# Reordering SyncE's transfers and the tap order of row-tiled matmuls in a deformable convolution kernel

## The chip, the cores and the metric
The kernel runs on one core of one Trainium2 chip. The time is that of one execution on the device, in microseconds, as a median over runs.

## What is computed
The input x has 8 images of 32 channels and 128x128 pixels, float32. Two blocks are applied one after the other, each to the group-normalised x (32 groups of one channel, so mean and variance of each channel of each image), and each adds its result to x.

```python
x  = x  + L0(_gn(x))    # depthwise 3x3, then three channel mixes (two of them softmax matrices)
x1 = x
x  = x1 + L1(_gn(x1))
# L1: off = conv3x3(v, w_off)               64 channels: a row and a column offset per pixel and channel
#     mapped = bilinear sample of v at grid + off, clipped to the image
#     conv3x3(mapped, w_conv) + b_conv
```

## The kernel before
**Stages.** L0 is folded into one 3x3 convolution, conv1, whose result x1 stands in `x1a` (three buffers, one per image in turn). Then come the offsets (`offsets`), the sampling in 8 chunks of an image (`deform` on VectorE, `offset_parts` on ScalarE, the chunk loop on GpSimd), and conv2 on the sampled image, which VectorE adds to `x1a`; from there it is stored. The image index is i, a step s takes two of the 8 chunks, so an image has four steps.

**TensorE.** In each step it first runs `offsets(i, s)` and then the jobs of `jobs_behind`: conv1 of image i+1 in steps 0 and 1 (four groups each, `x1`), conv2 of image i-1 in steps 2 and 3 (`c2`). A job waits in `wait_freed` until the PSUM bank that it takes has been read. The fourth conv1 group takes the bank of the first. In images 0, 1 and 7 the jobs are spread in another way.

**Offsets (L801 to L823).** A matmul takes one row group r (32 partitions of x1a, one image row in four) and one half t of the output's partitions, so there are eight tiles (r, t). For each of three ky, nine taps in all, kx is the outer loop and the rotated row groups are the inner one. At ky > 0 the row group r adds to what r - 1 wrote, so L813 waits for that row group's last matmul of the ky before, on one of four semaphores.

**SyncE's queue, in program order (L554 to L617).** For image i: copy mapa's first half to mapb (`copy_mapb(0)`, 2 DMAs); store half 1 of image i-2 (4 DMAs, L461 and L464); move the sampled rows of half 1 into mapa (`move_mapa(1)`, 16 DMAs) and copy them to mapb; load xb of image i+2 (8 DMAs); wait for x1's pads and move both halves of image i+1's strips (`move_strips`, 16 DMAs a half); `move_mapa(0)`, as soon as conv2 of image i-1 has done four groups; store half 0 of image i-1 (5 DMAs) after six groups were added. An image's first conv2 group waits for both halves of mapa and mapb (L765 to L769).

**What hangs on it.** `x1_group` (L957) must not overwrite `x1a` before the image that it held is stored: group 0 of image i+1 waits for half 0 of image i-2. `clamp(i, 1)` fills the borders of the strips' half 1 and `row_steps(i, 2)` and `(i, 3)` on GpSimd subtract its rows; chunks 4 to 7 read them. `STORE_AFTER` is the count of added groups at which a half may be stored, `CONV2_GROUPS` the order of conv2's groups; group g writes blocks 4g to 4g+3 of 32, and half 0 of mapa is what the even groups read.

Of the kernel before, what the change touches and what calls it, by code (L numbers as in the profile page):

```python
# [13 lines left out]
def deformable_preact_kernel(nc, x, dw_w, pw_w, att_w, glob_w, off_w, conv_w, conv_b, out):  # L14
# [15 lines left out]
    NK = HQ // KR  # L30
# [17 lines left out]
    NS = NK // 2  # L48
# [9 lines left out]

    BANKS = ["", "c", "xc", "xyc", "cxyc", "ycxyc"]

    CONV2_GROUPS = [0, 2, 4, 6, 1, 3, 5, 7]
    STORE_AFTER = [6, 8]
    BEFORE_END_GROUPS = [1, 2, 3, 0, 4, 5, 6, 7]


# [5 lines left out]
    def spread(i):  # L71
        return isinstance(i, int) and NB - 2 <= i < NB
# [77 lines left out]
    with ctx:  # L150
# [6 lines left out]
        def sem(name):  # L157
            return ctx.enter_context(nc.semaphore(name))
# [134 lines left out]
        mapped_pads = sem("mapped_pads")  # L293
# [13 lines left out]
        first2_done = sem("first_group_of_conv2_done")  # L307
        x1_ready = sem("x1_ready")
        off_done = [sem(f"off_done_side{n}") for n in range(2)]
        row_step = [sem(f"row_step_of_rows{n}") for n in range(4)]  # L310
        off_used = sem("off_used")
        parts_ready = sem("parts_ready")
        cols_ready = sem("cols_ready")
# [5 lines left out]
        mapped_ready = sem("mapped_ready")  # L319
        conv2_done = sem("conv2_done")  # L320
# [118 lines left out]
        def move_strips(queue, i, half):  # L439
            for strip in range(4):  # L440
                move_strip(queue, i, half, strip)
# [33 lines left out]
        def _(sp):  # L475
# [27 lines left out]
            def move_mapa(half):  # L503
                move_rows(mapa, 4 * half, 4, mapa_moved[half])
# [49 lines left out]
            for i in range(NB):  # L554
                prev, nxt, after = i >= 1, i + 1 < NB, i + 2 < NB
                if prev:

                    if i == 1:
                        move_strips(sp, i, 1)
                    sp.wait_ge(map_pads, i)  # L560
                    sp.wait_ge(mapa_moved[0], A_MOVES * DMA * i)
                    copy_mapb(0)
                if nxt and i >= 2:
                    sp.wait_ge(out_ready, 8 * (i - 1))
                    store(sp, i - 2, (i - 2) % 3, 1)
                if prev:
                    sp.wait_ge(mapped_ready, NK * i)
                    if i >= 2:
                        sp.wait_ge(conv2_done, 8 * (i - 1))
                    sp.wait_ge(mapped_pads, 2 * i)  # L570
                    move_mapa(1)
                    sp.wait_ge(mapa_moved[1], A_MOVES * DMA * i)
                    copy_mapb(1)
                if after and prev:
                    for half in range(2):

                        sp.wait_ge(conv1_done, 8 * (i + 1) + (5 if half == 0 else 8))
                        load_xb(i + 2, half, xb_loaded)
                if not prev:
                    sp.wait_ge(mapped_ready, 4)  # L580
                    sp.wait_ge(s_setup["dve"], 6)
                    sp.wait_ge(mapped_pads, 1)
                    move_mapa(0)
                if nxt:

                    sp.wait_ge(x1_pads, i + 2)
                    sp.wait_ge(mapped_ready, NK * i + 4)
                    for half in range(2 if prev else 1):
                        move_strips(sp, i + 1, half)
                if not nxt:  # L590
                    if i >= 2:
                        sp.wait_ge(out_ready, 8 * (i - 1))
                        for part in range(2):
                            store(sp, i - 2, (i - 2) % 3, part)
                    sp.wait_ge(end_pads, 1)
                    sp.wait_ge(mapped_pads, 2 * i + 1)
                    sp.wait_ge(mapped_ready, NK * i + 4)
                    move_rows(xa, 0, 4, end_moved[0])
                    sp.wait_ge(end_moved[0], A_MOVES * DMA)
                    copy_rows(xb, xa, 0, 4, end_copied)  # L600
                    sp.wait_ge(mapped_pads, 2 * i + 2)
                    sp.wait_ge(mapped_ready, NK * i + 6)
                    move_end_rows((0, 1), FULL, end_moved[1])
                    sp.wait_ge(mapped_ready, NK * i + 7)
                    move_end_rows((2, 3), LEFT, end_moved[1])
                    sp.wait_ge(out_ready, 8 * i)
                    for part in range(2):
                        store(sp, i - 1, (i - 1) % 3, part)
                    break
                if prev:  # L610
                    sp.wait_ge(mapped_ready, NK * i + 4)
                    sp.wait_ge(conv2_done, 8 * (i - 1) + 4)
                    sp.wait_ge(mapped_pads, 2 * i + 1)
                    move_mapa(0)
                if prev and after:
                    sp.wait_ge(out_ready, 8 * (i - 1) + STORE_AFTER[0])
                    store(sp, i - 1, (i - 1) % 3, 0)  # L617


            for m in (1, 3, 5):  # L620
# [48 lines left out]
        def _(pe):  # L669
# [131 lines left out]
            def offsets(i, wpar, par, s, tiles):  # L801


                half, parity = s // 2, s % 2
                for ky in range(3):
                    order = [(3 + ky + n) % 4 for n in range(4)]
                    for kx in range(3):
                        for r in order:
                            c = (r - ky) % 4
                            side, n, shift = c % 2, c // 2, (c + ky) // 4  # L810
                            if ky > 0 and kx == 0:

                                pe.wait_ge(row_step[(r - 1) % 4], 4 * (NS * i + s) + 2 * ky)  # L813
                            for t in range(2):
                                b = 2 * NJ * t + NJ * half + parity + shift
                                last = nc.tensor.matmul(tiles[side][64 * t:64 * t + 64, CH * n:CH * n + CH],  # L816
                                                        wo[wpar][Q * r:Q * r + Q, 3 * ky + kx, :],
                                                        x1a[par][Q * r:Q * r + Q, b:b + 7:2, kx:kx + W],
                                                        start=(ky == 0 and kx == 0), stop=(ky == 2 and kx == 2))
                                if kx == 2 and ky < 2:  # L820
                                    last.then_inc(row_step[r], 1)
                                elif kx == 2:
                                    last.then_inc(off_done[side], 1)  # L823

# [44 lines left out]
        def _(act):  # L869
# [193 lines left out]
            for i in range(NB):  # L1063
                prev, nxt = i >= 1, i + 1 < NB
                for s in range(NS):
# [25 lines left out]
                    sum_far(i, b)  # L1091
                    if s == 0:
                        pad_mapped(i, i % 3, 0)
                        clamp(i, 1)
                    if s == 1 and not nxt:
                        pad_end(i % 3)
# [53 lines left out]
        def _(pool):  # L1150
# [62 lines left out]
            for i in range(NB):  # L1213
                for k in range(NK):
# [20 lines left out]
                    if i >= 1 and k % 4 == 0:  # L1235
                        pool.wait_ge(mapa_moved[k // 4], A_MOVES * DMA * i)
                    pool.tensor_tensor(mapped_of_chunk(k), split(side), split(column),  # L1237
                                       ALU.add).then_inc(mapped_ready, 1)
                    if k in (1, 3):
                        row_steps(i, 2 + k // 2)  # L1240
                    elif k >= NK - 2 and i + 1 < NB:
                        row_steps(i + 1, k % 2)

# [379 lines left out]
```

## Time and profile before
| what | value |
|---|---|
| median of 3 runs | 734.21 us (733.68 to 735.55) |
| profiled execution | 738.19 us, span on the core 736.3 us |
| granted TensorE clock, mean | 0.959 of full |
| TensorE, VectorE, GpSimd, ScalarE busy | 89%, 72%, 65%, 61% of the span |
| chain that ended last | TensorE 39%, SyncE's queue 21%, ScalarE 7%, VectorE 6% |
| offsets (L816) | 4608 matmul records, 289.2 us busy |

L12 is line 12 of the kernel. PEld is TensorE's loading of weights. SPq is SyncE issuing DMAs: the engine is held while it issues one. Every matmul of float32 shows as two records, each with its own weight load, so the 72 matmuls of a block of offsets are 144 records. PEclk is the granted share of TensorE's full clock of 2.4 GHz. The ends of matmuls are modelled, so their starts are what to read.

### The profile page before, as it was taken

The page shows a single profiled execution, that of the slowest core. Times are in us where ns is not written, and L with a number is a line of the kernel's source. Part 1 is how long each engine was busy: PE and PEld are TensorE (multiplying, and loading weights), DVE is VectorE, ACT ScalarE, POOL GpSimd, SP SyncE. Part 2 cuts the span into 40 slices and gives each one's busy share as a digit, 9 for nine tenths or more (in the row PEclk, how much of TensorE's full clock was granted, in tenths as well). Part 3 has the DMA queues.
Part 4 walks back from the last instruction along what each step waited for, and adds up shares of the span by engine and source line. Part 5 has one row for each costly group of instructions (what it writes and reads, how often), then busy time and mean ns, then how long its engine had stood idle before and what let it go on. Part 6 is the DMA issues. An engine that isn't in the chain of part 4 may idle for free.

```text
span 736.3 us, 16859 instructions
## 1 busy us (share of the span) xinstructions
PE 655.6 (89%) x6572; PEld 297.2 (40%) x6572; DVE 528.4 (72%) x1027; ACT 451.1 (61%) x778; POOL 478.8 (65%) x412
## 2 busy tenths in 40 slices
PE   4799877888996999889997999989997999789965
PEld 4334433344442444434442444433443444344422
DVE  3686987558894688828886488848987386567872
ACT  7236757676754766556665766548656666576740
POOL 4013746969687476857768376876768476977650
PEclk9999999989998999989998999999999999989989
DMA  8958723589348894498747894498945623457555
GB/s 143 186 112 152 117 59 75 137 165 160 75 105 192 176 171 115 120 210 164 141 107 168 179 201 103 106 208 174 154 114 140 145 60 77 106 126 184 128 125 130
DMA packets 135413, 101.40 MB, mean 138 GB/s; under 512 B 13696, under 2 KB 112544, under 8 KB 135328
## 3 DMA queue, kind: packets, MB, share of 16 engines
q1 hardware_dynamic: 111296, 88.47, 57.6%
q10 hardware_dynamic: 24032, 11.78, 9.6%
q8 instruction: 54, 0.88, 0.6%
q14 instruction: 31, 0.25, 0.1%
HBM read 31.59 MB, written 16.78 MB: 66 GB/s over the span
## 4 chain that ended last, share of the span: by engine, by line
PE 39%; SPq 21%; ACT 7%; DVE 6%; issue 5%; POOL 5%; DMA 2%; ACTq 1%; DVEq 0%; POOLq 0%
PE off_ps L816 21%; SPq L429 11%; PE c_ps L698 9%; PE off_ps L698 7%; SPq L500 7%; DMA out_dram<-x1a 2%; DVE other_row L1426 2%; ACT off_abs L1010 2%; SPq L461 1%; ACT down_ps L1008 1%; ACT beyond L1020 1%; ACT other_row L997 1%; SPq L464 1%; DVE xb L1504 1%; POOL other_col L1231 1%
## 5 line engine op out<-in xcount | busy, mean ns | idle before, releaser
L816 PE MATMUL off_ps<-x1a,wo 32*64 32x512 f32 x4608 | 289.2, 611 | 22.6 <-ACT x1a L965 12.4
L816 PEld LDWEIGHTS off_ps<-x1a,wo 32*64 32x64 f32 x4608 | 162.1, 133 | 149.8 <-issue 65.7
L1426 DVE COPY_PREDICATED other_row<-down_ps,row_diff 128x768 f32<-128x768 int32 x128 | 124.6, 1027 | 117.5 <-ACT down_ps L1008 117.5
L997 ACT ACTIVATE other_row<-row_diff 128x768 f32<-128x768 f32 x128 | 101.1, 839 | 57.9 <-POOL row_diff L1207 26.3
L1223 POOL TENSOR_TENSOR other_row<-other_row,x_strips 128x512 f32<-128x512 f32 x48 | 57.2, 1192 | 118.2 <-DVE other_row L1440 118.2
L1224 POOL TENSOR_TENSOR other_col<-other_col,other_row 128x512 f32<-128x512 f32 x64 | 87.8, 1372 | 43.6 <-DVE other_row L1440 43.6
L1008 ACT ACTIVATE down_ps<-off_ps,bias_o 128x512 f32<-128x512 f32 x64 | 42.0, 655 | 100.3 <-PE off_ps L816 85.9
L698 PE MATMUL off_ps<-xb,w 128*64 128x512 f32 x198 | 90.3, 605 | 8.2 <-DVE xb L1504 7.0
L698 PE MATMUL c_ps<-xb,w 128*64 128x512 f32 x138 | 74.5, 682 | 22.0 <-ACT x1a L965 22.0
L700 PE MATMUL off_ps<-xa,w 128*64 128x512 f32 x198 | 90.3, 605 | 0.0
L1231 POOL TENSOR_TENSOR other_col<-other_col,off_abs 128x512 f32<-128x512 f32 x64 | 82.8, 1294 | 5.0
L698 PE MATMUL off_ps<-mapb,w 128*64 128x512 f32 x192 | 85.9, 595 | 0.0
L1228 POOL TENSOR_TENSOR other_col<-other_col,other_row 128x512 f32<-128x512 f32 x64 | 81.9, 1279 | 5.0
L1237 POOL TENSOR_TENSOR mapped<-other_col,other_row 128x512 f32<-128x512 f32 x64 | 81.7, 1277 | 5.0
L1205 POOL TENSOR_TENSOR row_diff<-x_strips 128x792 f32<-128x792 f32 x32 | 52.9, 1653 | 45.9 <-ACT x_strips L1039 45.9
L700 PE MATMUL off_ps<-mapa,w 128*64 128x512 f32 x168 | 75.0, 595 | 0.0
L1020 ACT ACTIVATE beyond<-off_abs,minus_one 128x1024 bf16<-128x1024 f32 x64 | 73.3, 1145 | 2.0
L700 PE MATMUL c_ps<-xa,w 128*64 128x512 f32 x138 | 74.5, 682 | 0.0
L1010 ACT ACTIVATE off_abs<-off_ps,bias_o 128x1024 f32<-128x1024 f32 x64 | 71.0, 1110 | 0.0
L698 PE MATMUL c_ps<-mapb,w 128*64 128x512 f32 x144 | 65.9, 593 | 0.0
L1382 DVE BATCH_NORM_STATS2 stats<-x1a 128x6 f32<-128x512 f32 x64 | 40.7, 681 | 34.7 <-ACT x1a L965 34.7
L700 PE MATMUL c_ps<-mapa,w 128*64 128x512 f32 x126 | 57.7, 593 | 0.0
(160 smaller groups left out, 1059.9 us busy)
## 6 DMA issues: line engine op xcount, KB each, us to landing
mapa<-mapped SPq DMA_DIRECT2D x224, 65.0 KB, 2.1
mapb<-mapa SPq DMA_DIRECT2D x28, 520.0 KB, 6.4
out_dram<-x1a SPq DMA_DIRECT2D x49, 256.0 KB, 4.7
xb<-in_x_dram SPq DMA_DIRECT2D x48, 256.0 KB, 10.6
xa<-in_x_dram ACTq DMA_DIRECT2D x40, 256.0 KB, 7.4
x_strips<-x1a SPq DMA_DIRECT2D x112, 81.2 KB, 2.1
x_strips<-x1a SPq DMA_DIRECT2D x112, 65.0 KB, 2.0
xa<-in_x_dram SPq DMA_DIRECT2D x16, 256.0 KB, 6.5
```

The costliest lines, as they stand in the source:

```text
L429: queue.dma_start(to[p_to:p_to + Q, at:at + n * WP], x1a[par][p:p + Q, b:b + n, :].rearrange("p b w -> p (b w)")) .then_inc(strips_loaded[ ...
L698: nc.tensor.matmul(bank[0:64, :], weights[:, kx, :], rows_b[:, of, kx:kx + W], start=(kx == 0), stop=(kx == 2))
L700: last = nc.tensor.matmul(bank[64:128, :], weights[:, kx, :], rows_a[:, of, kx:kx + W], start=(kx == 0), stop=(kx == 2))
L816: last = nc.tensor.matmul(tiles[side][64 * t:64 * t + 64, CH * n:CH * n + CH], wo[wpar][Q * r:Q * r + Q, 3 * ky + kx, :], x1a[par][Q * r:Q ...
L997: act.activation(other_row[n][:, :, KR // 2 * odd:KR // 2 * odd + KR // 2, :], diff_of_chunk(k, odd), ACT.Copy)
L1010: act.activation(off_abs[n][:, :], off[:, :], ACT.Abs, bias=bias_o[i % 2][:, 0:1]).then_inc(abs_ready, 1)
L1020: act.activation(beyond[:, :], off_abs[k % 2][:, :], ACT.Relu, bias=minus_one[:, :], accum_out=far[i % 2][:, k:k + 1]).then_inc(beyond_rea ...
L1224: step(pool.tensor_tensor(side, side, other_row[n][:, 0, :, :], ALU.add))
L1228: step(pool.tensor_tensor(side, side, column, ALU.subtract))
L1231: step(pool.tensor_tensor(side, side, off_abs[n][:, 1:2 * CH:2].rearrange("p (h w) -> p h w", h=KR), ALU.mult))
L1237: pool.tensor_tensor(mapped_of_chunk(k), split(side), split(column), ALU.add).then_inc(mapped_ready, 1)
L1426: last = dve.copy_predicated(other_row[n][:, :, KR // 2 * odd:KR // 2 * odd + KR // 2, :], bass.AP(tensor=rows.tensor, offset=rows.offset ...
```

## The change
SyncE: half 1 of the strips is no longer moved along with half 0 at the end of the image before, but in the image itself, after the store of image i-2. At the end of the iteration the store of half 0 now comes ahead of `move_mapa(0)`; the store waits for four added groups and not six, `move_mapa(0)` for six groups of conv2 and not four. conv2's groups come in an order that finishes half 0 of the image first. ScalarE does `clamp(i, 1)` at the end of step 1 and not of step 0, and GpSimd `row_steps(i, 2)` after chunk 2 and not chunk 1. TensorE: for each ky one wait for all eight tiles, on one semaphore, and then for each row group all three kx for both t.

```diff
--- before.py
+++ after.py
@@ -58,8 +58,9 @@
 
     BANKS = ["", "c", "xc", "xyc", "cxyc", "ycxyc"]
 
-    CONV2_GROUPS = [0, 2, 4, 6, 1, 3, 5, 7]
-    STORE_AFTER = [6, 8]
+    CONV2_GROUPS = [0, 2, 1, 3, 4, 6, 5, 7]
+    STORE_AFTER = [4, 8]
+    HALF_READ = 6
     BEFORE_END_GROUPS = [1, 2, 3, 0, 4, 5, 6, 7]
 
 
@@ -307,7 +308,7 @@
         first2_done = sem("first_group_of_conv2_done")
         x1_ready = sem("x1_ready")
         off_done = [sem(f"off_done_side{n}") for n in range(2)]
-        row_step = [sem(f"row_step_of_rows{n}") for n in range(4)]
+        row_step = sem("row_step")
         off_used = sem("off_used")
         parts_ready = sem("parts_ready")
         cols_ready = sem("cols_ready")
@@ -554,9 +555,6 @@
             for i in range(NB):
                 prev, nxt, after = i >= 1, i + 1 < NB, i + 2 < NB
                 if prev:
-
-                    if i == 1:
-                        move_strips(sp, i, 1)
                     sp.wait_ge(map_pads, i)
                     sp.wait_ge(mapa_moved[0], A_MOVES * DMA * i)
                     copy_mapb(0)
@@ -564,6 +562,7 @@
                     sp.wait_ge(out_ready, 8 * (i - 1))
                     store(sp, i - 2, (i - 2) % 3, 1)
                 if prev:
+                    move_strips(sp, i, 1)
                     sp.wait_ge(mapped_ready, NK * i)
                     if i >= 2:
                         sp.wait_ge(conv2_done, 8 * (i - 1))
@@ -585,8 +584,7 @@
 
                     sp.wait_ge(x1_pads, i + 2)
                     sp.wait_ge(mapped_ready, NK * i + 4)
-                    for half in range(2 if prev else 1):
-                        move_strips(sp, i + 1, half)
+                    move_strips(sp, i + 1, 0)
                 if not nxt:
                     if i >= 2:
                         sp.wait_ge(out_ready, 8 * (i - 1))
@@ -607,14 +605,13 @@
                     for part in range(2):
                         store(sp, i - 1, (i - 1) % 3, part)
                     break
-                if prev:
-                    sp.wait_ge(mapped_ready, NK * i + 4)
-                    sp.wait_ge(conv2_done, 8 * (i - 1) + 4)
-                    sp.wait_ge(mapped_pads, 2 * i + 1)
-                    move_mapa(0)
                 if prev and after:
                     sp.wait_ge(out_ready, 8 * (i - 1) + STORE_AFTER[0])
                     store(sp, i - 1, (i - 1) % 3, 0)
+                if prev:
+                    sp.wait_ge(conv2_done, 8 * (i - 1) + (4 if spread(i - 1) else HALF_READ))
+                    sp.wait_ge(mapped_pads, 2 * i + 1)
+                    move_mapa(0)
 
 
             for m in (1, 3, 5):
@@ -803,14 +800,13 @@
 
                 half, parity = s // 2, s % 2
                 for ky in range(3):
-                    order = [(3 + ky + n) % 4 for n in range(4)]
-                    for kx in range(3):
-                        for r in order:
+                    if ky > 0:
+
+                        pe.wait_ge(row_step, 16 * (NS * i + s) + 8 * ky)
+                    for r in range(4):
+                        for kx in range(3):
                             c = (r - ky) % 4
                             side, n, shift = c % 2, c // 2, (c + ky) // 4
-                            if ky > 0 and kx == 0:
-
-                                pe.wait_ge(row_step[(r - 1) % 4], 4 * (NS * i + s) + 2 * ky)
                             for t in range(2):
                                 b = 2 * NJ * t + NJ * half + parity + shift
                                 last = nc.tensor.matmul(tiles[side][64 * t:64 * t + 64, CH * n:CH * n + CH],
@@ -818,7 +814,7 @@
                                                         x1a[par][Q * r:Q * r + Q, b:b + 7:2, kx:kx + W],
                                                         start=(ky == 0 and kx == 0), stop=(ky == 2 and kx == 2))
                                 if kx == 2 and ky < 2:
-                                    last.then_inc(row_step[r], 1)
+                                    last.then_inc(row_step, 1)
                                 elif kx == 2:
                                     last.then_inc(off_done[side], 1)
 
@@ -1091,6 +1087,7 @@
                     sum_far(i, b)
                     if s == 0:
                         pad_mapped(i, i % 3, 0)
+                    if s == 1:
                         clamp(i, 1)
                     if s == 1 and not nxt:
                         pad_end(i % 3)
@@ -1236,8 +1233,8 @@
                         pool.wait_ge(mapa_moved[k // 4], A_MOVES * DMA * i)
                     pool.tensor_tensor(mapped_of_chunk(k), split(side), split(column),
                                        ALU.add).then_inc(mapped_ready, 1)
-                    if k in (1, 3):
-                        row_steps(i, 2 + k // 2)
+                    if k in (2, 3):
+                        row_steps(i, k)
                     elif k >= NK - 2 and i + 1 < NB:
                         row_steps(i + 1, k % 2)
```

## Rows read from the trace of the kernel before
**Rows 1.** The page's chain that ended last, by line.
```profile
PE off_ps L816 21%; SPq L429 11%; PE c_ps L698 9%; PE off_ps L698 7%; SPq L500 7%; DMA out_dram<-x1a 2%; DVE other_row L1426 2%; ACT off_abs L1010 2%; SPq L461 1%; ACT down_ps L1008 1%; ACT beyond L1020 1%; ACT other_row L997 1%; SPq L464 1%; DVE xb L1504 1%; POOL other_col L1231 1%
```
**Rows 2.** Busy us of PE, PEld, DVE, ACT, POOL, then PEclk, DMA, GB/s: image 4.
```profile
378.58:463.62 85.04, 80.56 (x818) 35.61 (x816) 63.08 (x124) 53.56 (x93) 59.97 (x49) 0.96 0.76 155
```
**Rows 3.** Waits over the run: who waited for whom: us, times, longest.
```profile
ACT x1a L962 <- DMA out_dram<-x1a: 18.1, 5, 5.2
PE c_ps L698 <- ACT x1a L965: 22.0, 6, 6.0
PEld off_ps L816 <- PE off_ps L816: 54.7, 64, 1.7
```
**Rows 4.** ScalarE and TensorE by time in image 4: start, length, instruction.
```profile
398.98 0.36 ACT L962 ACTIVATE x1a<-c_ps,bias 32x128 f32<-32x128 f32 x1 [3.07 <-DMA out_dram<-x1a]
...
399.96 1.12 PE L698 MATMUL c_ps<-xb,w 128*64 128x512 f32 x1 [3.78 <-ACT x1a L965]
```
**Rows 5.** Columns of rows 2, for the conv1 group behind that gap.
```profile
315.19:320.58 5.39, 5.39 (x20) 1.31 (x23) 1.86 (x3) 2.22 (x4) 5.16 (x5) 0.50 0.98 218
484.77:489.09 4.32, 4.32 (x20) 1.21 (x23) 1.86 (x3) 2.22 (x4) 4.16 (x4) 0.64 0.97 211
```
**Rows 6.** SyncE's DMA issues by time, from image 3's third step on.
```profile
358.82 22.03 SPq L429 DMA_DIRECT2D x_strips<-x1a  x32
380.97 10.82 SPq L500 DMA_DIRECT2D mapa<-mapped  x16
391.83 2.28 SPq L461 DMA_DIRECT2D out_dram<-x1a  x3
...
420.86 0.64 SPq L514 DMA_DIRECT2D mapb<-mapa  x1
```
**Rows 7.** TensorE by time: conv2's fifth group, and its first one image later.
```profile
368.15 0.62 PE L698 MATMUL c_ps<-mapb,w 128*64 128x512 f32 x1
...
433.70 0.51 PE L709 MATMUL c_ps<-mapb,w 128*32 128x384 f32 x1
```
**Rows 8.** VectorE by time: the addition of conv2's fourth group, image 3.
```profile
360.92 0.74 DVE L1410 SCALAR_TENSOR_TENSOR x1a<-c_ps,bias,x1a 128x512 f32<-128x512 f32 x1
```
**Rows 9.** L514 with its landings, and SyncE's wait for moved rows.
```profile
L514 SPq DMA_DIRECT2D mapb<-mapa x14: 632/637/643, 138.1 to 663.0; - x14
...
DMA to landing us min/median/max: 6.4/6.6/11.7
...
SPq L513 <- DMA mapa<-mapped: 12.0, 7, 2.6
```
**Rows 10.** TensorE by time: two rounds of conv2, then one block of offsets.
```profile
292.50 0.59 PE L698 MATMUL c_ps<-mapb,w 128*64 128x512 f32 x1
...
292.93 0.59 PE L698 MATMUL c_ps<-mapb,w 128*64 128x512 f32 x1
...
293.45 8.84 PE L816 MATMUL off_ps<-x1a,wo 32*64 32x512 f32 x144
```
**Rows 11.** Weight loads in 293.45 to 293.52, 296.30 to 296.42 and 296.30 to 296.50.
```profile
293.45 0.19 PEld L816 LDWEIGHTS off_ps<-x1a,wo 32*64 32x64 f32 x10 [0.81 <-issue]
...
L816 PEld LDWEIGHTS off_ps<-x1a,wo 32*64 32x64 f32 x4 | 0.2, 130 | 0.9 <-PE off_ps L816 0.9
...
L816 PEld LDWEIGHTS off_ps<-x1a,wo 32*64 32x64 f32 x8 | 0.3, 129 | 0.9 <-PE off_ps L816 0.9
```
**Rows 12.** Weight loads by time at the tail of image 3's first conv1 group.
```profile
304.59 0.11 PEld L717 LDWEIGHTS c_ps<-xb,w 128*32 128x32 f32 x1 [0.20 <-issue]
...
304.70 0.11 PEld L713 LDWEIGHTS c_ps<-xb,w 128*32 128x32 f32 x1
```
**Rows 13.** GpSimd and ScalarE by time in image 4, steps 1 and 3.
```profile
425.21 1.28 POOL L1237 TENSOR_TENSOR mapped<-other_col,other_row 128x512 f32<-128x512 f32 x1
...
427.57 1.58 ACT L997 ACTIVATE other_row<-row_diff 128x768 f32<-128x768 f32 x2 [0.70 <-issue]
...
453.20 0.66 ACT L1008 ACTIVATE down_ps<-off_ps,bias_o 128x512 f32<-128x512 f32 x1 [5.21 <-PE off_ps L816]
```

## The prediction, made before the changed kernel ran
> **What bounds the kernel now.** I read the chain that ended last first: TensorE's matmuls are its largest part, and SyncE's issuing of two transfers, the strips (L429) and mapa (L500), comes next with 18% of the span [rows 1]. The busy times by image say the same: of 85.0 us TensorE is busy 80.6, VectorE 63.1, GpSimd 60.0 and ScalarE 53.6 [rows 2]. So an image costs TensorE's work plus its gaps, and the waits show where these are. TensorE waits 22.0 us for ScalarE's copies of conv1, and ScalarE waits 18.1 us, five times, before L962 for a store to land [rows 3]: group 0 of conv1 may not overwrite an image that is not yet stored. In image 4 ScalarE starts L962 at 398.98 after 3.07 us of waiting, and TensorE goes on at 399.96 after a gap of 3.78 us [rows 4].
>
> The gap costs more than its length. The group behind it takes 5.39 us with a granted clock of 0.50, which is the lower level of 1.2 GHz; TensorE was idle ahead of it. A group is six rounds of 0.43 us [rows 10], 2.6 us. There are five such groups, three of 5.3 to 5.4 us and two of 4.3 to 4.5 [rows 5], together 24.9 us where 13.0 would do: 11.9 us, or 2.4 an image.
>
> **The change part by part.** *The store of half 0.* Before, its first DMA is issued at 391.83, behind 32 strip moves (22.03 us) and 16 mapa moves (10.82 us) [rows 6]. VectorE has added the fourth group at 361.66 already [rows 8], and with the new group order that is all half 0 needs. The store now follows 16 strip moves, half of 22.03 us, so it goes out at about 358.8 + 11.0 = 369.9, some 22 us sooner. ScalarE's wait then ends at once: L962 would start at 398.98 - 3.07 = 395.91, TensorE 0.98 us later at 396.89, and it arrives there at 396.18. A gap of 0.7 us stays, with ScalarE itself as its cause. I take it that the clock doesn't fall for so short a gap. TensorE's side of the gain is 18.1/5 + 2.4 = 6.0 us in each of images 2 to 6.
>
> *What is late next: SyncE's queue.* From the first strip move at 358.82 to the last mapb copy at 420.86, SyncE issues nearly without a stop, and that copy lands 6.6 us after its issue [rows 6, 9], at 427.5. conv2 of that image starts at 433.70 and needs it [rows 7], so the slack is 6.2 us. The change takes no DMA out of this stretch: the 16 strip moves of half 1 leave its start and come back ahead of `move_mapa(1)`. It adds one landing: `copy_mapb(0)` now stands right behind `move_mapa(0)`, where the store's five issues had covered it. The like of it, mapb copy behind mapa moves, is 12.0/7 = 1.7 us, at most 2.6 [rows 9]; I take 2.1. TensorE can then gain 6.2 - 2.1 = 4.1 us an image until conv2 waits for the copy; the rest of its 6.0 us turns into that wait. There is a second coupling. `move_mapa(0)` now waits for conv2's sixth group. The fifth starts at 368.15 [rows 7], so the sixth is done at about 368.15 + 5.2 = 373.4, and SyncE comes by at 369.9 + 4.9 (five store issues) = 374.8. Those 1.4 us of cover are gone wherever conv2 itself started late. I take off 0.5 us an image for that, with 0 and 1.4 as its ends. Net 3.6 us, five times: 18.0 us.
>
> *The other moves.* Behind the waiting `move_mapa(0)` stand both mapb copies and `move_mapa(1)`; all that waits for them is conv2, which is counted. The strips' half 1 is issued at about 394 to 405 instead of before 381. Its reader, `clamp(i, 1)`, moves to the end of ScalarE's step 1, just ahead of the L997 at 427.57 [rows 13]. On GpSimd `row_steps(i, 2)` now stands behind chunk 2, whose last operation ends at 426.49. It waits there about 1 us for the clamp and takes 2.5 us, and chunk 3 and ScalarE's copies for chunk 5 come some 3 us later than before. In the next steps ScalarE waits 5.21 us for TensorE [rows 13], which hides it; without that cover it would cost up to 3 us an image. I cost these moves at nothing.
>
> *The offsets.* A block is 144 records in 8 tiles, 18 rounds of 0.43 us, and takes 8.84 us [rows 10]. 18 x 0.43 = 7.74, the modelled tail of the last matmul is 0.16 more, and 0.94 us stay for the two borders between ky, 0.47 each. Now each row group waits for itself: at a border the first four loads are there by 296.42 and the next four only by 296.50 [rows 11], so four waits spread the tiles over some 0.25 us, while at a block's start ten loads begin within 0.07 us. One wait for all starts the tiles together, but waits for the last of them, which ends 0.05 us after the first. I estimate 0.15 us a border, 0.3 a block, with nothing and 0.47 a border as the ends. In images 2 to 6 SyncE's queue bounds, so this buys nothing there; in images 0, 1 and 7 most of it disappears into waits. I count 0.5 us in all.
>
> That holds if the eight tiles still run side by side. All six records of a tile's ky now come in one go, twelve for a row group, and the last row group's first load stands behind 36 matmul records. The tiles run together only if the engine goes past matmuls that are waiting. It does so to some depth. At 304.59 a weight load of L717 starts, while a load of L713, earlier in the program, starts at 304.70 [rows 12]; at that moment each of three tiles still had two passes to start, so a tile holds at least three, the running one included. The new order wants six. The Trainium skill, TensorE: Matmul & The Clock Gate (Part 3, packing small matmuls), says otherwise: matmuls start and end strictly in program order and only weight loads are pulled ahead. By that rule row groups would follow one another here, which is a rival below. Rows 11 speak against it: four loads, the second passes of both tiles among them, start ahead of the third tile's wait at a border, and at a block's start the first passes of all tiles start before any second one.
>
> **The sum.** 736.3 - 18.0 - 0.5 = 717.8 us span. The profiled execution took 738.19 us, 0.5% above the median of 734.21, so I take the difference off the median: 715.7 us.
>
> **The rivals.** *SyncE's queue eats the gain.* If the strip moves behind a store and mapb copies are slowed, or the exposed landing is nearer 6 us, the 6.2 us of slack are spent and TensorE waits at conv2 for what it no longer waits for at conv1. For it: SyncE is 18% of the chain [rows 1] and the DMA engines are busy for 0.76 of an image [rows 2]. Against: no transfer is added. With half of the gain, 725; with all of it lost, 734. The other way, if SyncE never bounds, 5 x 6.0 and 0.3 us for some 20 blocks come off: 698.
>
> *The tiles fall out of step (slower).* Say a tile holds n passes, the running one included. A row group's last record can be placed when 6 - n of its passes are done, so each of the three later row groups of a ky starts (6 - n) x 0.43 us behind the one ahead. With n = 3, the least that rows 12 allow, that is 3 x 3 x 1.29 = 11.6 us a block, 371 us for 32 blocks: about 1090 us. With n = 5 it is 3.9 us a block, 124 us, about 845. With a common window in which only the last row group comes one round late, 3 x 0.43 = 1.3 us a block, 41 us less the gain of 18: about 757. It decides from 18/32 = 0.56 us a block. No row shows a tile with more than two passes waiting, for or against. The rule of the skill in this kernel is the case of one row group after another: with no pass held, about 3 x 3 x 6 x 0.43 = 23 us a block more, some 740 us in all.
>
> *The change doesn't do what it says.* The store goes out early but another wait stands in the same place, 734.
>
> **How the numbers follow.** The forecast has a chance of 0.66 (706 to 727), the queue that eats most of the gain 0.13 (727 to 737), no effect 0.03. Slower: the last row group one round late 0.06 (745 to 765), tiles well out of step, n of 5 or less, 0.09, and strict program order 0.02; 0.01 for the clamp's or another wait. The range from 706 to 738 holds 0.81. A measurement of this kernel tells a change of about 0.3% from none, 2.2 us: faster 0.77, same 0.05, slower 0.18.
>
> **What would show it.** Right: the wait of L962 for the store is gone, the group behind it takes 2.6 us, and a block of offsets takes 8.4 to 8.8 us in 18 rounds. A new wait of TensorE for mapb at L698 or L709, near 2 us in each of images 2 to 6, is the mark of SyncE's bound. Wrong: a block over 9.4 us, with the records of one row group ahead of the next; or a wait at conv2 of 5 us and more; or ScalarE waiting at L997 for GpSimd's row_diff on the way to a gap of TensorE.

## Result and the profile after

| | before | after |
|---|---|---|
| median of 4 runs | 734.88 us (733.68 to 738.15) | 1128.46 us (1105.15 to 1143.57) |
| profiled execution, span | 738.19 us, 736.3 us | 1113.57 us, 1111.7 us |
| granted TensorE clock, mean | 0.959 | 0.823 |

The changed kernel is slower: ratio 1.51, 95% interval 1.502 to 1.518. The ratio is that of the two faster of its four runs, 1105 and 1114 us; the other two took 1143 us at a lower mean clock. The forecast was 715.7 us, with a range of 706 to 738. The page of after, first the span, then TensorE's granted clock in 40 slices (tenths of full), the chain that ended last by line, and the two costliest groups (busy us, mean ns of one, idle time ahead of it and what ended that):

```profile
span 1111.7 us, 16859 instructions
...
PEclk9969566856789699699789699697899796958878
...
PE off_ps L812 60%; PE off_ps L695 16%; PE c_ps L695 12%; PE c_ps L706 2%; PE c_ps L710 1%; PE off_ps L706 1%; PE off_ps L710 1%; DVE xb L1501 1%; PE off_ps L721 0%; PE c_ps L714 0%; DVE other_row L1423 0%; ACT off_abs L1006 0%; ACT down_ps L1004 0%; PE off_ps L697 0%; PE off_ps L714 0%
...
L812 PE MATMUL off_ps<-x1a,wo 32*64 32x512 f32 x4608 | 683.5, 740 | 11.9 <-DVE other_row L1437 4.8
L812 PEld LDWEIGHTS off_ps<-x1a,wo 32*64 32x64 f32 x4608 | 236.2, 154 | 443.1 <-issue 358.5
```

SyncE's strip and mapa moves, 18% of the chain in [rows 1], are gone from it. The offsets (L816 before, L812 now) are 60% of it where they were 21%. The same 4608 records kept TensorE busy for 289.2 us before and do so for 683.5 now, so the whole loss is there. Two blocks of offsets that follow each other, the last of image 2 and the first of image 3, as busy us of PE, PEld, DVE, ACT and POOL with counts, then PEclk, DMA share and GB/s:

```profile
415.67:432.58 16.91, 16.73 (x148) 6.50 (x148) 6.50 (x12) 2.96 (x5) 6.85 (x6) 1.00 0.54 132
443.08:467.96 24.88, 24.69 (x148) 8.09 (x148) 8.02 (x29) 5.28 (x11) 11.59 (x10) 0.66 0.60 141
```

A block took 8.84 us in [rows 10]. Now it takes 16.9 us at the full clock, in 15 of the 32 blocks, and 20.3 to 32.3 us where the clock is at 0.50 (1.2 GHz) for a part of it or all, in the other 17. From its first start to its last end, all 32 blocks add up to 290.8 us before and 689.4 us after, 398.6 more. That splits in two: 32 x (16.9 - 8.84) = 257.9 us come from the block being longer at the full clock, and 435.8 us in the 17 blocks against 17 x 16.9 = 287.3 are 148.5 us from the lower clock (together 406.4; before, the blocks had lost 7.9 us to it already, 290.8 - 32 x 8.84). Outside the blocks the span is 23.2 us shorter than before (422.3 against 445.5).

**Inside a block.** TensorE's weight loads by time at the start of the first of these blocks (start, length, instruction, count, idle time ahead):

```profile
415.66 0.19 PEld L812 LDWEIGHTS off_ps<-x1a,wo 32*64 32x64 f32 x4 [0.81 <-issue]
416.15 0.14 PEld L812 LDWEIGHTS off_ps<-x1a,wo 32*64 32x64 f32 x2 [0.30 <-issue]
416.58 0.20 PEld L812 LDWEIGHTS off_ps<-x1a,wo 32*64 32x64 f32 x6 [0.30 <-issue]
417.01 0.20 PEld L812 LDWEIGHTS off_ps<-x1a,wo 32*64 32x64 f32 x4 [0.23 <-issue]
417.44 0.27 PEld L812 LDWEIGHTS off_ps<-x1a,wo 32*64 32x64 f32 x8 [0.23 <-issue]
417.94 0.20 PEld L812 LDWEIGHTS off_ps<-x1a,wo 32*64 32x64 f32 x4 [0.23 <-issue]
418.37 0.27 PEld L812 LDWEIGHTS off_ps<-x1a,wo 32*64 32x64 f32 x8 [0.23 <-issue]
```

A tile's load for the next pass runs beside the pass before. The four loads at 415.66 are the first two passes of the first row group's two tiles, where [rows 11] had ten loads at once. The two at 416.15 are their third. The six at 416.58 are their fourth and the first two of the second row group. So the second row group starts when the first starts its third pass, ahead of the first one's fifth and sixth, which stand earlier in the program, and the next ones at 417.44 and 418.37, again 0.86 and 0.93 us later. At 416.58 each of the first two tiles has one pass running and three waiting (the fourth to the sixth), and only then does the engine take records that stand behind them. A tile holds four passes. In the prediction's formula n is 4: 3 x 3 x 2 x 0.43 = 7.7 us a block. With 0.3 us more for the one wait (below), 8.84 + 7.7 + 0.3 = 16.9.

That is also why the clock matters more. The second block, cut where the granted clock changes:

```profile
443.08:451.22 8.14, 8.05 (x74) 3.30 (x76) 7.02 (x27) 3.63 (x9) 7.94 (x7) 1.00 0.33 80
451.22:467.96 16.74, 16.65 (x82) 4.79 (x72) 1.00 (x3) 1.65 (x2) 3.65 (x3) 0.50 0.73 170
```

TensorE shows as busy throughout, but in the 8.14 us ahead of the fall it started 72 matmul records (two of the view's 74 had begun before), where the block of [rows 10] starts 144 in 8.84. The busy share alone, 96% of the span, hides both. In 15 of the 17 blocks the clock fell like this, 6.9 to 13.3 us behind the block's start, with TensorE idle for 0.2 us at most since then. In one block it fell 2.1 us behind the start, after 1.2 us of idle time, and one began at the lower clock.

### The profile page after: what moved, and what is told of

The parts are those of the page before. It is cut to its first block, busy times and chain, and to the rows that moved or that the text cites. A ratio compares the mean times of both kernels' runs of the same rounds, so it can differ in the third digit from the quotient of the medians.

```text
span 1111.7 us, 16859 instructions
## 1 busy us (share of the span) xinstructions
PE 1069.9 (96%) x6572; PEld 378.1 (34%) x6572; DVE 536.9 (48%) x1027; ACT 451.9 (41%) x778; POOL 476.9 (43%) x412
## 4 chain that ended last, share of the span: by engine, by line
PE 93%; DVE 2%; issue 2%; ACT 1%; DVEq 0%; ACTq 0%
PE off_ps L812 60%; PE off_ps L695 16%; PE c_ps L695 12%; PE c_ps L706 2%; PE c_ps L710 1%; PE off_ps L706 1%; PE off_ps L710 1%; DVE xb L1501 1%; PE off_ps L721 0%; PE c_ps L714 0%; DVE other_row L1423 0%; ACT off_abs L1006 0%; ACT down_ps L1004 0%; PE off_ps L697 0%; PE off_ps L714 0%
## 5 line engine op out<-in xcount | busy, mean ns | idle before, releaser
L812 PE MATMUL off_ps<-x1a,wo 32*64 32x512 f32 x4608 | 683.5, 740 | 11.9 <-DVE other_row L1437 4.8
L812 PEld LDWEIGHTS off_ps<-x1a,wo 32*64 32x64 f32 x4608 | 236.2, 154 | 443.1 <-issue 358.5
L695 PE MATMUL off_ps<-xb,w 128*64 128x512 f32 x198 | 94.2, 626 | 7.3 <-DVE xb L1501 7.3
L697 PE MATMUL off_ps<-xa,w 128*64 128x512 f32 x198 | 94.2, 626 | 0.0
L695 PE MATMUL off_ps<-mapb,w 128*64 128x512 f32 x192 | 93.8, 640 | 0.0
L697 PE MATMUL off_ps<-mapa,w 128*64 128x512 f32 x168 | 80.3, 629 | 0.0
L695 PE MATMUL c_ps<-mapb,w 128*64 128x512 f32 x144 | 71.4, 634 | 0.0
L695 PE MATMUL c_ps<-xb,w 128*64 128x512 f32 x138 | 70.6, 652 | 0.0
L697 PE MATMUL c_ps<-xa,w 128*64 128x512 f32 x138 | 70.6, 652 | 0.0
L697 PE MATMUL c_ps<-mapa,w 128*64 128x512 f32 x126 | 63.1, 640 | 0.0
```

What stands on the lines that cost most here:

```text
L695: nc.tensor.matmul(bank[0:64, :], weights[:, kx, :], rows_b[:, of, kx:kx + W], start=(kx == 0), stop=(kx == 2))
L697: last = nc.tensor.matmul(bank[64:128, :], weights[:, kx, :], rows_a[:, of, kx:kx + W], start=(kx == 0), stop=(kx == 2))
```

## The experiments

**1. SyncE's part alone, then with the one wait.** The changed kernel with TensorE's offsets as they were; the second with the one wait and row groups in plain order, kx still outside.

```diff
 # e1_sync_alone: after, and in offsets() again
+                    order = [(3 + ky + n) % 4 for n in range(4)]
+                    for kx in range(3):
+                        for r in order:
+                            if ky > 0 and kx == 0:
+                                pe.wait_ge(row_step[(r - 1) % 4], 4 * (NS * i + s) + 2 * ky)
 # e2_sync_one_wait: after, and
-                    for r in range(4):
-                        for kx in range(3):
+                    for kx in range(3):
+                        for r in range(4):
```

> The kernel after with TensorE's offsets as they were before: four waits a ky, kx outside, rotated row groups inside. Theory A (the tap order alone costs the 50%, and the moves on SyncE, ScalarE and GpSimd gain as predicted): the block of offsets is back at 8.84 us, ScalarE's wait for the store (18.1 us) is gone, the half-clock conv1 group behind it takes 2.6 us, TensorE waits up to about 2 us an image for mapb, and the time is 714 to 722 us. Rival B (the moves cost too, by a wait for the late strips or for mapb): 734 us or more.

> The kernel after with kx outside and the four row groups inside, not rotated; one wait for all tiles at each ky is kept. Theory A: 18 rounds, a block of 8.4 to 8.7 us, the time equal to that of e1 or up to 5 us below it. If the one wait were a part of the loss, the block would be over 9 us and the time above that of e1 by more than 5 us.

Measured: 740.2 us, ratio 1.0065 (1.0036 to 1.0094), a block 8.84 us; and 741.3 us, 1.0074 (1.0046 to 1.0101), a block 9.14. So the order of row groups and kx makes the loss, and SyncE's part is no gain even without it. What TensorE waited for in the first (us in total, times, longest), SyncE and ScalarE in the same kernel, and, from the end of image 4 into image 5, the start of conv2 and SyncE's issues:

```profile
PE c_ps L706 <- DMA mapb<-mapa: 16.0, 5, 6.6
...
PE c_ps L695 <- ACT x1a L962: 3.0, 5, 0.6
...
SPq L501 <- PE off_ps L697: 13.2, 3, 5.5
...
ACT other_row L994 <- POOL row_diff L1205: 58.6, 24, 4.8
```

```profile
433.75 0.82 PE L706 MATMUL c_ps<-mapb,w 128*32 128x384 f32 x1 [6.59 <-DMA mapb<-mapa]
...
440.20 10.07 SPq L430 DMA_DIRECT2D x_strips<-x1a  x16
450.32 2.24 SPq L462 DMA_DIRECT2D out_dram<-x1a  x3
...
454.08 1.18 SPq L467 DMA_DIRECT2D out_dram<-x1a  x1
460.88 11.36 SPq L501 DMA_DIRECT2D mapa<-mapped  x16
...
482.70 11.39 SPq L430 DMA_DIRECT2D x_strips<-x1a  x16
494.20 10.80 SPq L501 DMA_DIRECT2D mapa<-mapped  x16
507.67 0.66 SPq L514 DMA_DIRECT2D mapb<-mapa  x1
```

The 22.0 us at conv1 [rows 3] are down to 3.0, as forecast. In their place TensorE waits 16.0 us for mapb at conv2, up to 6.6 us at a time, and ScalarE 58.6 us for row_diff (26.3 before). SyncE stands still from 455.26 to 460.88, for conv2's sixth group. Rival B of the first expectation is what came. In the second the block is over 9 us, as feared, but the time is only 1.1 us above the first one's.

**2. The one wait, and the order of row groups, each alone.** Edits to the kernel before: all tiles on one semaphore and one wait ahead of each ky; and only the two loops swapped, with the four waits and the rotation kept. The swap was run twice.

```diff
 # e3_one_wait_alone
+                    if ky > 0:
+                        pe.wait_ge(row_step, 16 * (NS * i + s) + 8 * ky)
 # e4_rows_outer_alone, e5_rows_outer_again
-                    for kx in range(3):
-                        for r in order:
+                    for r in order:
+                        for kx in range(3):
```

> The kernel before with only the four waits of a ky made into one, its order of matmuls untouched. Theory A: a block of 8.4 to 8.7 us and 728 to 735 us, since most of what 32 blocks save stands ahead of waits for the store. The opposite, that four staggered waits hide more than they cost: a block over 8.9 us and 737 us or more.

> The kernel before with only the two loops changed: row group outside, kx inside, four waits and rotation kept. Theory A: the row groups start two passes (0.86 us to 0.93 us) behind one another, a block takes 16 to 18 us at full clock and up to 25 us where the clock is at its lower level, and the time is 1090 to 1150 us. Rival B, by which a good part of the loss comes from the moves on SyncE: below 1000 us.

> e4 once more, since its two executions were 859 and 1069 us apart. Theory G, that the stagger of the row groups alone gives 860 us and the lower clock the rest in some executions: executions in both places or between them, and blocks of 13.0 us at full clock in each profile, over 20 us where the granted clock is at its lower level.

Measured, one wait: 739.47 us, ratio 1.007 (1.0032 to 1.0107), a block 9.14 us. Its wait at the border, and the loads at a block's start and behind its first border:

```profile
PE off_ps L815 <- PE off_ps L815: 19.5, 64, 0.3
```

```profile
443.95 0.23 PEld L815 LDWEIGHTS off_ps<-x1a,wo 32*64 32x64 f32 x16 [0.81 <-DVE x1a L1409]
...
445.73 0.18 PEld L815 LDWEIGHTS off_ps<-x1a,wo 32*64 32x64 f32 x8 [0.26 <-issue]
447.09 0.24 PEld L815 LDWEIGHTS off_ps<-x1a,wo 32*64 32x64 f32 x16 [1.19 <-PE off_ps L815]
```

Two loads for each of the eight tiles start together, so all run side by side. The block is longer, not shorter, the opposite of what Theory A expected: at each of the 64 borders TensorE stands idle for 0.3 us, and no view of before shows such a wait. In the kernel before the row groups that are ready go on while the last one is still waiting.

Measured, loops swapped: 858.78 us with a mean granted clock of 0.943 in the profiled run, and 1069.09 us with 0.716 in the run beside it; the second time 869.75 us, ratio 1.174 (1.166 to 1.183). A block of it at the full clock and one at the lower clock:

```profile
408.10:421.10 13.00, 13.00 (x150) 5.92 (x152) 7.11 (x28) 3.91 (x6) 10.27 (x9) 1.00 1.27 184
98.40:122.53 24.13, 24.10 (x144) 8.45 (x144) 15.09 (x55) 5.02 (x8) 11.60 (x9) 0.51 0.19 45
```

Loads of the first one, at the start of the fourth row group of a ky and of the first of the next:

```profile
410.80 0.26 PEld L816 LDWEIGHTS off_ps<-x1a,wo 32*64 32x64 f32 x8 [0.23 <-issue]
...
411.72 0.26 PEld L816 LDWEIGHTS off_ps<-x1a,wo 32*64 32x64 f32 x8 [0.23 <-issue]
```

13.0 us stand between 8.84 and 16.9, not at the 16 to 18 us that Theory A expected; below 1000 us as Rival B had it, but not for its reason, since e1 shows what SyncE's part costs. With four waits and the rotation a row group waits at a border only for the one that it adds to, so the stagger of one ky runs on into the next: in this block the twelve row groups start 0.92 us apart all through, and 11 x 0.92 + 6 x 0.43 + 0.16 = 12.9. The one wait makes every ky run empty and start the stagger anew, three times a block: 16.9. So the swap alone costs about 130 us, and the one wait, which costs 3 to 5 us by itself, adds over 200 to it: 32 x 3.9 = 125 us of longer blocks, and most of the rest is the lower clock. The clock matters here too, in another way: three blocks of 32 were at 0.50 in the profiled run of 858.8 us, four in that of 871.3 us. In each run the last of them began so, and before the others TensorE had been idle for 2.1 to 2.8 us; it fell within 1.6 us of their start, never later in a block. But then it stayed down for 27 to 31 us, where a fall in the kernel before lasted 3.4 to 6.8. The run of 1069.1 us has no trace; why its clock was low is not shown, and none of the four later runs (858.7 to 872.0 us) came near it.

**3. How deep a tile's queue is, and whose it is.** Three orders with the one wait and SyncE's change (edits to e2), all with the same 144 records a block.

```diff
 # f1_two_taps_a_row_group: taps 0 and 1 of each row group, then tap 2
+  for kx, r in [(kx, r) for taps in ((0, 1), (2,)) for r in range(4) for kx in taps]:
 # f2_row_group_pairs: all taps of row groups 0 and 1, then of 2 and 3
+  for kx, r in [(kx, r) for pair in ((0, 1), (2, 3)) for kx in range(3) for r in pair]:
 # f3_tile_by_tile: all six passes of one tile, then of the next
+  for r in range(4):
+      for half_t, kx in [(t, kx) for t in range(2) for kx in range(3)]:
```

> e2 with taps 0 and 1 of a row group in a row (four passes a tile), for each row group, and then tap 2 of each. Theory A, that a tile holds four passes (one running, three waiting): nothing stops, 18 rounds, a block of 9.14 us as in e2, 736 to 745 us. Theory C, that the row groups overlap badly as soon as one of them has more than one matmul in a row: the block is 11 us or more.

> e2 with row groups 0 and 1 given all their three taps in turn, and then 2 and 3. Theory A: the second pair starts two passes late once a ky, 8 rounds and not 6, a block of 9.14 + 3 x 0.86 = 11.7 us at full clock. Theory D, one store of waiting passes shared by all tiles (the six that stood in the two tiles of a row group in the kernel after): four tiles share it, the second pair starts three or four passes late and the block is 13 us or more.

> e2 with row group outside, then half t, then the three taps: six passes in a row for one tile. Theory A, four passes held by each tile: each of the eight tiles starts two passes behind the one ahead, 20 rounds a ky, a block near 60 x 0.43 + 1 = 27 us at full clock, more where it falls, 1400 us or more in all. Theory E, that the eight places belong to a row group and both its tiles draw on them: the second tile starts at once and the block stays near the 16.9 us of the kernel after, 1100 to 1150 us.

| | median, us | ratio (interval) | block at the full clock, us |
|---|---|---|---|
| f1, four passes of a tile in a row | 742.34 | 1.012 (1.007 to 1.017) | 9.62 |
| f2, six in a row in four tiles | 785.63 | 1.071 (1.066 to 1.076) | 11.59 |
| f3, six in a row in one tile | 1908.28 | 2.600 (2.588 to 2.613) | none at the full clock; 44.8 at a mean of 0.60 |

Four passes in a row are free but for 0.5 us, six are not. Loads of f1 late in its first ky, then of f2 and of f3 from a block's start:

```profile
402.45 0.15 PEld L812 LDWEIGHTS off_ps<-x1a,wo 32*64 32x64 f32 x3 [0.22 <-issue]
402.88 0.44 PEld L812 LDWEIGHTS off_ps<-x1a,wo 32*64 32x64 f32 x13 [0.28 <-issue]
```

```profile
446.83 0.21 PEld L812 LDWEIGHTS off_ps<-x1a,wo 32*64 32x64 f32 x8 [0.81 <-issue]
447.31 0.15 PEld L812 LDWEIGHTS off_ps<-x1a,wo 32*64 32x64 f32 x4 [0.28 <-issue]
447.74 0.23 PEld L812 LDWEIGHTS off_ps<-x1a,wo 32*64 32x64 f32 x12 [0.28 <-issue]
```

```profile
55.47 0.19 PEld L812 LDWEIGHTS off_ps<-x1a,wo 32*64 32x64 f32 x2
55.95 0.13 PEld L812 LDWEIGHTS off_ps<-x1a,wo 32*64 32x64 f32 x1 [0.30 <-issue]
56.38 0.19 PEld L812 LDWEIGHTS off_ps<-x1a,wo 32*64 32x64 f32 x3 [0.30 <-issue]
...
57.24 0.24 PEld L812 LDWEIGHTS off_ps<-x1a,wo 32*64 32x64 f32 x4 [0.25 <-issue]
...
58.16 0.24 PEld L812 LDWEIGHTS off_ps<-x1a,wo 32*64 32x64 f32 x4 [0.25 <-issue]
```

In f2 four tiles run, and the other four begin at 447.74 (12 loads: the fourth passes of the first four, and two each for the new ones), 0.91 us behind, once a ky: 9.14 + 3 x 0.86 = 11.7, measured 11.59. In f3 a new tile begins at 56.38, 57.24 and 58.16, each when the one ahead starts its third pass, though it had stood free until then. So the four passes are counted for each tile: Theory A holds in f2 and f3. A store that all tiles share, or one for each row group (of eight passes, by after's count), would have taken the first tile's six and let its neighbour start at once. Seven such steps of 0.9 us in each of three ky, 18.9 us, on 9.14 give 28 us at the full clock; the clock did the rest: 28 us at a mean clock of 0.60 would be 47, and 44.8 were measured. f1's last 0.16 us a ky is not explained: a tile there has exactly four passes in a row, yet of the eight loads for fifth passes only three come at 402.45, and the other five a round late.

**4. Is it the number of increments on one semaphore?** The kernel before with its four semaphores, but all four waits ahead of the ky.

```diff
 # g1_four_waits_ahead
+                    if ky > 0:
+                        for r in order:
+                            pe.wait_ge(row_step[(r - 1) % 4], 4 * (NS * i + s) + 2 * ky)
```

> The kernel before with its four waits and four semaphores kept, but all four ahead of a ky's first matmul. If the 0.30 us that one wait costs a block comes from waiting for all eight tiles before any starts: a block of 9.1 to 9.4 us and 736 to 742 us. If it comes from eight increments of one semaphore: below 9.0 us, at the time of the kernel before.

Measured: 745.21 us, ratio 1.016 (1.011 to 1.022), a block 9.35 us. With four semaphores the block is not shorter but 0.2 us longer than with one. Idle time at a border is 0.4 us (26.1 us in 64 waits). So the eight increments on one semaphore are not what costs; that nothing starts until everything is done is the account that is left.

**5. What of SyncE's part is worth having.** In the kernel before, only the store of half 0 ahead of `move_mapa(0)`; then also the store of half 1 ahead of `copy_mapb(0)`; then the first with the new order of conv2's groups, the store after four of them and mapa's wait for six, but the strips, `clamp` and `row_steps` where they were.

```diff
 # h1_store_first
+                if prev and after:
+                    sp.wait_ge(out_ready, 8 * (i - 1) + STORE_AFTER[0])
+                    store(sp, i - 1, (i - 1) % 3, 0)
                 if prev:
 ...
                     move_mapa(0)
-                if prev and after: (the same three lines)
 # i1_strips_as_before: the same, and
+    CONV2_GROUPS = [0, 2, 1, 3, 4, 6, 5, 7]
+    STORE_AFTER = [4, 8]
-                    sp.wait_ge(conv2_done, 8 * (i - 1) + 4)
+                    sp.wait_ge(conv2_done, 8 * (i - 1) + (4 if spread(i - 1) else HALF_READ))
```

> The kernel before with one swap on SyncE: the store of half 0 ahead of move_mapa(0). Groups, counts, clamp and strips as before. Theory F (the gain of the moves was eaten by SyncE's queue and by move_mapa(0) waiting for conv2's sixth group): the wait for the store is gone, move_mapa(0) never waits for conv2, one landing of 1.5 to 2 us is exposed, TensorE waits for mapb by less than 2.5 us an image, 712 to 725 us. If the moved transfers themselves are what costs, 734 us or more.

> h1 with the store of half 1 of image i-2 also ahead of the first mapb copy, so that it covers the landing of mapa. Theory F: TensorE's waits for mapb fall by 1.5 to 2 us an image against h1, 705 to 720 us and below h1. If that copy is no part of the bound, the same time as h1.

> The kernel before with SyncE's change except the strips: new order of conv2's groups, store of half 0 after four added groups and ahead of the mapa moves, which wait for conv2's sixth group; both halves of the strips are moved together as before, and clamp and row_steps stay in their old steps. TensorE's offsets are as before. It stands between the swap of store and mapa alone (ratio 0.9845) and SyncE's change in full (1.0065), which differ by 16 us. Theory A, the wait for the sixth group loses it: SyncE again waits up to 5.5 us for conv2 ahead of mapa, TensorE waits for mapb in most images, ratio 1.000 to 1.010. Theory B, the moved strips lose it: with both halves ahead of the store SyncE reaches mapa 11 us later, after conv2's sixth group, so that wait is nearly nothing, and ScalarE's waits for row_diff fall back from 58.6 to about 26 us; ratio 0.980 to 0.992. Both in part: 0.992 to 1.000.

Measured: 723.98 us, ratio 0.985 (0.981 to 0.988); 723.1 us, 0.984 (0.980 to 0.988); 724.24 us, 0.985 (0.981 to 0.989). All three are faster than both kernels, by some 12 us than the one before, with blocks of 8.84 us. The second is no faster than the first, so the copy that it covers is no part of the bound. TensorE's waits in h1, and SyncE's issues in i1 over the stretch shown for e1:

```profile
PE c_ps L709 <- DMA mapb<-mapa: 10.1, 2, 5.3
...
PE c_ps L698 <- ACT x1a L965: 5.1, 7, 1.1
```

```profile
436.10 21.12 SPq L430 DMA_DIRECT2D x_strips<-x1a  x32
457.27 2.20 SPq L462 DMA_DIRECT2D out_dram<-x1a  x3
...
462.33 12.40 SPq L501 DMA_DIRECT2D mapa<-mapped  x16
...
484.87 12.22 SPq L501 DMA_DIRECT2D mapa<-mapped  x16
498.57 0.65 SPq L514 DMA_DIRECT2D mapb<-mapa  x1
```

i1 differs from e1 in the strips with their `clamp` and `row_steps` (and in a wait of SyncE's for mapped rows that the kernel before has), and that makes 16 us (1.0065 against 0.985). With all strip moves in front, SyncE reaches mapa's moves at 462.2, when conv2's sixth group is done, and does not stop. In e1 it is there at 455.3 and stops for 5.6 us, and still has half of the strips to move before `move_mapa(1)`. The copy that conv2 waits for goes out at 498.57 in one and at 507.67 in the other, 9.1 us apart. 4.1 us of this e1 had already at its first strip move (440.20 against 436.10), and the other 5.0 are about the stop: the DMAs in this stretch are the same. Theory B is what came; SyncE waits for no conv2 group ahead of mapa's moves, and ScalarE's waits for row_diff are 28.9 us instead of 58.6. How the 16 us come about is shown in part only. The profiled spans differ by 13.9 us; TensorE's waits for mapb make 6.5 of it (17.7 us against 11.2) and its longer busy time 5.2, with 57 us at the lower clock against 47. Whether the strips or the later `row_steps` weigh more was not taken apart. conv2's new order, store threshold and wait by themselves are worth nothing here (i1 against h1).

## Why the prediction was wrong

- *Failed: that the eight tiles still run side by side.* The prediction made the gain hang on it and read [rows 12] as a tile holding at least three passes. That was right as a bound. The number is four, and the new order wants six. The second rival, tiles out of step, is what happened; its formula gives 8.84 + 7.7 us for n = 4, and 16.9 less the 0.3 us of the wait is 16.6. The rival got a chance of 0.09 because rows 11 showed records passing one another. But they showed it for an order that hands a tile two passes at a time, and the step to six was taken without a row. For n = 3 the price at the full clock, 371 us, is near the 375 us measured by accident: 258 us are the blocks at the full clock, 141 more are the lower clock, which the prediction priced for no case but its gaps, and 23 came off elsewhere.
- *Failed in sign: the one wait.* The estimate was 0.15 us less at each border. It is 0.15 us more (9.14 against 8.84). The spread of 0.25 us in [rows 11] is not lost time. It is row groups that start as soon as the one they add to is done, and a wait for all gives this up.
- *Right: the store.* ScalarE's wait before L962 is gone and the gap at conv1 is 0.6 us (0.7 forecast) in e1, and the clock does not fall for it: the group behind runs at 1.00 (396.25 to 398.90). But in e1 it now falls behind waits for mapb, at 0.50 from 431.49 to 438.32 for one, and the lower clock holds for 57 us of the run, where it held for 61 before. The like of the gap is 5.1 us in seven waits in h1, where 22.0 stood.
- *Wrong: what the moved strips cost.* "The other moves" were put at nothing, and SyncE's stretch was said to hold the same DMAs as before. It does, but 16 of them had been the cover under which SyncE waited for conv2's groups. The prediction took 1.4 us of cover for the sixth group to be left and capped the loss at that. In e1 SyncE waits up to 5.5 us there, at 455.26 for groups of conv2 whose first had itself begun 6.59 us late for want of mapb: one image's late copy delays the next one's. Such late starts alone are not it: h1 has two (5.3 and 4.7 us) and i1 too (6.4 and 4.8), and SyncE does not stop behind them. With TensorE's part left out, the first rival is what happened, in full: 734 forecast for it, 740.2 measured in e1. The trace of before had both parts, mapa moves behind 32 strip moves [rows 6] and the group that they would wait for [rows 7].
- *Right in size, in another kernel:* 18.0 us were forecast for the store, 11.8 us by the medians and 12.5 by the profiled spans came with h1. Two waits of about 5 us for mapb remain there, above the 2.5 us an image that were expected.
- *The strict order.* The Trainium skill, TensorE: Matmul & The Clock Gate (Part 3, packing small matmuls), has matmuls start and end in program order. In after the first matmuls of the second row group start at 416.59, and the fifth passes of the first, which stand earlier in the program, at 417.44, so this doesn't hold between tiles; between those of one tile it does here. The page also gives a reorder window of 64 for the engine. Here 12 matmuls with their 12 loads were enough to hold up the next row group for 0.92 us, so in this kernel that depth was not what set the limit.

## What to carry to other kernels

Where small matmuls run side by side in tiles, give the tiles their passes in turn (here at most four of one tile in a row, which are two fp32 matmuls), and let each tile wait only for what it adds to. A TensorE that shows as busy can be running two tiles where eight would fit, so compare how many records start in a microsecond, not busy shares. When transfers are moved out of a queue's stretch, ask which wait they were covering, and put the urgent store ahead without moving anything else first.

## What the runs showed of the hardware

- Each tile of TensorE holds four passes of 32x512, one running and three waiting; a record that finds its tile full stops everything behind it, loads for idle tiles included (after, f2 and f3 agree; f1 is within 0.16 us a ky).
- The granted clock fell to 0.50 inside 15 of the 32 blocks of after although TensorE had not been idle for more than 0.2 us since the block's start; ahead of one fall it had started 72 records in 8.14 us. In the blocks of e4 and e5 (13.0 us) it fell only within 1.6 us of a start, behind 2.1 to 2.8 us of idle time. In all, TensorE was at 0.50 for 61 us before, 39 in f2, 126 in e5, 394 in after and 1342 of 1910 in f3.
- Starting all tiles on a common wait leaves TensorE idle for 0.3 us at each border with one wait and 0.4 with four, and makes a block 0.3 and 0.5 us longer.
